# Reordering the layers stage of a two-layer block: four shifts in a row, gate sums ahead of the last head turnings, the next norm's statistics behind them

## The reference, cut to what matters

```python
# layer 0: attention in segments of 512 tokens, each against every 8th key (64 keys), 16 heads of 16
q4 = q.reshape(B, H, S, SEG, hd)
k4 = k.reshape(B, H, S, SEG, hd)[:, :, :, ::DIL]
scores = jnp.einsum('bhspd,bhskd->bhspk', q4, k4)
c = jnp.max(scores.reshape(B, H, S, nb, BLOCK_M, Kn), axis=4, keepdims=True)   # over 64 queries
w = jnp.exp(scores - c)
out = num / den[..., None]            # num = w v, den = sum of w
# layer 0: gate, an fp8 linear layer of the same normed tokens
out = jnp.einsum('bsi,oi->bso', x_dq, w_dq) + bias
...
x = x + s * g
xn = _layernorm(x, axis=-1)
# layer 1: q, k, v projections; q and k are rotated
q_rot = jnp.concatenate([q1 * cos - q2 * sin, q1 * sin + q2 * cos], axis=-1)
```

## Time and profile before

| what | value |
|---|---|
| median of 3 runs | 3221.84 us |
| the profiled execution's own time | 3216.31 us |
| its span | 3214.5 us |
| mean granted TensorE clock, of full speed | 0.971 |
| PE, DVE, ACT, POOL busy, share of the span | 90%, 79%, 64%, 21% |
| layers stage, segments 2 to 15 | from 128.5 us, one every 41.0 to 41.1 us |

### The profile page before, as it was taken

How to read it: one execution, slowest core, us unless ns; L and a number is a source line. 1 busy time by engine, 2 the same in 40 slices (tenths; PEclk the granted TensorE clock), 3 DMA queues, 4 the chain that set the end, 5 groups by cost and what they waited for, 6 DMA issues and landing times. The chain is left out here.

```text
span 3214.5 us, 66525 instructions
## 1 busy us (share of the span) xinstructions
PE 2893.3 (90%) x26519; PEld 1757.1 (55%) x26520; DVE 2555.0 (79%) x3560; ACT 2044.4 (64%) x3430; POOL 674.3 (21%) x1035
## 2 busy tenths in 40 slices
PE   5888888872899999999999999999899999999987
PEld 3555555550334443344344434434388888888975
DVE  4888888877899999999999999999265665666567
ACT  2555555540699999999999999999732232333234
POOL 1333333341222322000000000000132343332300
PEclk9999999985899999999999999999999999999999
DMA  2223333325223112222220122202121222212349
GB/s 76 69 86 89 88 91 93 93 86 102 51 55 54 36 24 54 54 54 53 54 53 17 43 54 54 53 22 87 52 68 34 71 80 73 68 42 70 103 150 309
DMA packets 252583, 230.21 MB, mean 72 GB/s; under 512 B 60908, under 2 KB 234988, under 8 KB 252012
## 3 DMA queue, kind: packets, MB, share of 16 engines
q1 hardware_dynamic: 235896, 192.32, 22.9%
q0 software_dynamic: 16384, 33.64, 3.3%
HBM read 124.21 MB, written 101.06 MB: 70 GB/s over the span
## 5 line engine op out<-in xcount | busy, mean ns | idle before, releaser
L1746 ACT ACTIVATE at_ex<-at_so,keep_exp_scale 128x512 f32<-128x512 f32 (+1 forms) x2304 | 1336.3, 679 | 203.6 <-PE at_so L1582 115.8
L1784 DVE TENSOR_REDUCE at_best<-at_p 128x2 f32<-128x1024 f32 (+3 forms) x1280 | 1284.5, 1060 | 111.1 <-PE at_p L1602 80.9
L1621 PE MATMUL at_so<-at_qs,at_ks 50*128 50x512 f16 (+3 forms) x2560 | 734.3, 352 | 33.0 <-ACT at_ex L1746 32.6
L1602 PE MATMUL at_p<-at_ks,at_qs 48*128 48x512 f16 (+3 forms) x2560 | 681.4, 358 | 50.6 <-DVE at_best L1784 49.4
L1692 PE MATMUL at_so<-at_ex,at_vs 128*32 128x256 f32 (+2 forms) x8704 | 697.2, 392 | 0.0
L2020 ACT ACTIVATE e_hh<-e_hb,e_b1now 128x512 fp32r<-128x512 f32 x256 | 176.4, 689 | 519.0 <-PE e_hb L1954 504.6
L1621 PEld LDWEIGHTS at_so<-at_qs,at_ks 50*128 50x128 f16 x2560 | 208.2, 93 | 517.6 <-ACT at_ex L1746 339.4
L1257 POOL DMA_INDIRECT e_xg<-s_xn,e_token x128 | 143.4, 1121 | 1359.5 <-DVE e_token L1252 1235.0
L1984 PE MATMUL e_ob<-e_w2h,e_hh 128*128 128x256 f32 x1024 | 295.3, 288 | 15.1 <-DVE e_og L2091 15.1
L1986 PE MATMUL e_ob<-e_w2h,e_hl 128*128 128x256 f32 x1024 | 291.8, 285 | 0.0
L1985 PE MATMUL e_ob<-e_w2l,e_hh 128*128 128x256 f32 x1024 | 291.7, 285 | 0.0
(11 more groups left out here) (267 smaller groups left out, 4498.6 us busy)
## 6 DMA issues: line engine op xcount, KB each, us to landing
s_v<-a_v SPq DMA_DIRECT2D x64, 256.0 KB, 3.0
s_qk<-a_part SPq DMA_DIRECT2D x128, 128.0 KB, 2.4
at_vs<-s_v SPq DMA_DIRECT2D x32, 512.0 KB, 10.3
s_eo<-at_empty SPq DMA_DIRECT2D x16, 1024.0 KB, 7.6
e_w<-w SPq DMA_DIRECT2D x16, 1024.0 KB, 7.7
f_rows<-s_eo SPq DMA_DIRECT2D x32, 512.0 KB, 8.0
at_qs<-s_qk SPq DMA_DIRECT2D x96, 128.0 KB, 4.4
at_ks<-s_qk SPq DMA_DIRECT2D x96, 128.0 KB, 7.2
```

The costliest lines, as they stand in the source:

```text
L1602: last = pe.matmul(out, qs[rows, buf, p, qt * P:(qt + 1) * P], ks[rows, buf, p, ch * SEG:ch * SEG + w], start=True, stop=ch != qc)
L1621: last = pe.matmul(so[:, v % NST, at:at + w], ks[rows, r, p, kt * P:(kt + 1) * P], qs[rows, r, p, q0:q0 + w], start=True, stop=not diag)
L1746: ev.done(act.activation(ex[:, v % NE, 0:width], so[:, v % NST, 0:width], ACT.Exp, scale=keep["exp_scale"][:, 0:1]), "ex")
L1784: last = dve.tensor_reduce(best[:, row:row + PAIRS * TT + 1:PAIRS * TT, ch], p1[:, at % NP1, :, to:to + w], AX, ALU.max)
```

## The change: what it does

The diff moves steps in the hand-written orders of POOL, PE, ACT and DVE. No instruction is added or taken away, and no buffer, shape or semaphore changes.

- DVE: all four `shift`s come first; `quantise_rest` moves behind `normalise(m, 0)`; `low_tokens(n)` behind `normalise(m, 1)`; `gated(m, 0)` and `gated(m, 1)` each one `normalise` earlier; `first_norm(m + 1)` behind `normalise(m, 3)`, right ahead of `residual(m, 0)`.
- PE: `scores(m, 3)` ahead of `turn_second(n)`; `gate(m, 0)` and `gate(m, 1)` each ahead of a `turn`; `project1(n, 2)` ahead of `turn_first(m + 1)`.
- ACT: `second_turned(n)` from behind `out_copy(m, 0)` to behind the third exponential, ahead of `out_copy(m, 1)`; `projected(n, 1)` ahead of `first_normed(m + 1)`; `projected(n, 2)` ahead of `first_turned(m + 1)`.
- POOL: `rotate` waits for the first `shift` of segment `n + 2` in place of `quant`; `rest(m - 2)` comes ahead of `inverse_root(m + 1, 0)`.

```diff
--- before.py
+++ after.py
@@ -350,7 +350,7 @@
                     ev.wait(pool, "pjc", n, 4)
                     ev.wait(pool, "p2", n, 0)
                     if n + 2 < NSEG:
-                        ev.wait(pool, "quant", n + 2, 1)
+                        ev.wait(pool, "shift", n + 2, 1)
                     st.then(pool.tensor_tensor(rot[:, :, 1, :], qk[:, :, 0, :], sin, ALU.mult))
                     st.then(pool.tensor_tensor(prod1[:], qk[:, :, 1, :], cos, ALU.mult))
                     st.settle()
@@ -385,10 +385,9 @@
                 for m in range(NSEG):
                     if m >= 2:
                         rotate(st, m - 2)
+                        rest(st, m - 2)
                     if m + 1 < NSEG:
                         inverse_root(st, m + 1, 0, "var", "rstd", "xn")
-                    if m >= 2:
-                        rest(st, m - 2)
                     inverse_root(st, m, 1, "var1", "rstd1", "xn1")
                 rotate(st, NSEG - 2)
                 rest(st, NSEG - 2)
@@ -589,25 +588,25 @@
                     for d in range(3):
                         scores(m, d)
                     values(m, 0)
+                    scores(m, 3)
                     if n >= 0:
                         turn_second(n)
-                    scores(m, 3)
                     values(m, 1)
                     turn(m, 0)
                     values(m, 2)
                     turn(m, 1)
                     values(m, 3)
+                    gate(m, 0)
                     turn(m, 2)
-                    gate(m, 0)
+                    gate(m, 1)
                     turn(m, 3)
-                    gate(m, 1)
                     project1(n, 0)
                     turn_heads(m)
                     project1(n, 1)
                     project(m)
+                    project1(n, 2)
                     if more:
                         turn_first(m + 1)
-                    project1(n, 2)
                     values1(n, 0)
                     project1(n, 3)
                     if more:
@@ -745,10 +744,10 @@
                         ev.wait(act, "shift", m, d + 1)
                         ev.wait(act, "pv", m, max(2 * (d - 1), 0))
                         ev.done(act.activation(wexp[:, d % 2], shifted[:, d % 2], ACT.Exp, scale=SCALE), "wexp")
+                        if d == 2 and n >= 0:
+                            second_turned(n)
                         if d >= 1:
                             out_copy(m, d - 1)
-                        if d == 1 and n >= 0:
-                            second_turned(n)
                     if n >= 1:
                         part0(n - 1)
                     out_copy(m, 3)
@@ -756,14 +755,14 @@
                     half_tanh(m, 1)
                     projected(n, 0)
                     heads_turned(m)
+                    projected(n, 1)
                     if more:
                         first_normed(m + 1)
                     if m == 0:
                         high_weights()
-                    projected(n, 1)
+                    projected(n, 2)
                     if more:
                         first_turned(m + 1)
-                    projected(n, 2)
                     logits(n, 0)
                     projected(n, 3)
                     if more:
@@ -1002,19 +1001,19 @@
                     n, more = m - 1, m + 1 < NSEG
                     shift(st, m, 0)
                     shift(st, m, 1)
+                    shift(st, m, 2)
+                    shift(st, m, 3)
+                    normalise(st, m, 0)
                     quantise_rest(st, m)
-                    shift(st, m, 2)
-                    normalise(st, m, 0)
-                    shift(st, m, 3)
+                    normalise(st, m, 1)
                     if n >= 0:
                         low_tokens(st, n)
-                    normalise(st, m, 1)
+                    gated(st, m, 0)
+                    normalise(st, m, 2)
+                    gated(st, m, 1)
+                    normalise(st, m, 3)
                     if more:
                         first_norm(st, m + 1)
-                    normalise(st, m, 2)
-                    gated(st, m, 0)
-                    normalise(st, m, 3)
-                    gated(st, m, 1)
                     residual(st, m, 0)
                     if n >= 1:
                         rest(st, n - 1)
```

## The result

The changed kernel takes 3259.52 us, the median of 4 runs (3257.85 to 3267.98), beside 3221.58 us for the kernel before in 4 runs (3220.45 to 3222.61): 1.0123 times, 95% interval 1.0105 to 1.0142. It is slower, 37.9 us by the medians. My forecast was 3236 us with a range up to 3254: the direction was right, the loss was more than twice as large, and the time lies outside the range. It fits the rival in which the clock falls in every segment (3242 to 3262), which I had given 0.14.

What follows compares the result with a forecast made beforehand. No single engine full in the layers stage; PE sets the pace in a segment's second half. Segments +7.8, clock +11.7, ends -5.2 gave +14.3 us, so 3236 us; own range 3229 to 3243, whole range 3209 to 3254.

Steps and rivals of the forecast that it cites:

- the rival in which the clock falls in every segment: TensorE's clock falls in all 13 steady segments, 1.3 to 2.9 us each: 3242 to 3262 us; chance 0.14.
- The first half of a segment: Shifts through projection on DVE and PE: `x1` added from 24.87 in place of 27.78, 2.9 us won on this path.
- POOL's chain: Next norm's inverse root on POOL: DVE instructions with two SBUF inputs hold three of its instructions up; ready at 26.71.
- The clock: PE's 3.4 us gap ahead of `turn_first` lowers the clock: 1.3 us in 9 of 13 segments, +11.7 us.
- 0.60: Loss per segment at full clock: `keys` start at 31.85 in place of 31.25; 13 segments make +7.8 us.
- The ends: Segments 0, 1 and 15 gain 1.4, 1.2 and 2.6 us, together -5.2.
- the clock stays up: Rival: the gap ahead of `turn_first` costs no clock, only +7.8 - 5.2 = +2.6: 3224 us; chance 0.18.
- POOL isn't caught: Rival: the inverse root gets through between DVE's instructions: 3189, or 3213 if only line 945 is missed; chance 0.18.
- the rotation meets `quantise_rest`: Rival: POOL's rotation runs 0.8 later, DVE stands up to 2.4 us: up to +30, 3250 us; chance 0.04.
- open in the prediction: Whether line 853 (statistics, one SBUF input) holds POOL up: nothing to two waits of about 0.3 each; taken as nothing.

Runs made afterwards that it cites:

- e1: The changed kernel with DVE's `rest` of segment n-1 moved behind `second_norm`: 0.9937 times the kernel before, a steady segment 39.99 us.
- e2: The changed kernel with 12 extra matmuls on PE behind `project1(n, 2)`, filling the gap: 1.0023 times the kernel before, a steady segment 42.00 us.
- e3: The changed kernel with `first_norm(m + 1)` put back behind `low_tokens`, ahead of the gate sums: 0.9921 times the kernel before, a segment 39.94 us.
- e6: The kernel of e3 with POOL's rotation waiting for `quant` again: 3281.8 us in one run, segments 46.6 and 45.5 us in turn.
- e7: The kernel before with only POOL's rotation waiting for the first shift instead of `quant`, one run: a segment 44.37 us.
- e4: The kernel before with only `first_norm(m + 1)` moved behind `gated(m, 1)`: 1.0363 times the kernel before, segments 49.01 and 49.96 us in turn.

## Why the prediction was right or wrong

*The first half of a segment* came as predicted: the fourth shift with a wait of 0.22, the first normalise at 9.94 (said: 9.90), the first gate sum at 14.71 (14.6), the statistics at 17.75 (17.77), line 944 at 24.78 (24.87). Line 932 fell to 1.22 and gave nothing. The rotation lay beside the shifts at 2.37 each.

*POOL's chain* was right in its mechanism and in its size: the three instructions are caught, and the chain ends at 26.90 where I had 26.71, since line 944 came a little earlier and catches the eleventh instruction instead of the twelfth. e1 shows this cause by experiment, and segment 1 by itself: without the collision of line 972 the chain ends 2.0 us earlier, and so clear of line 944.

*The clock* is the step that failed. I took 1.3 us in 9 of 13 segments, 11.7 us; it is 2.4 us (e2: 44.37 less 42.00) in 13 of 13, about 31 us. Both factors were too small. The 1.3 was read from segment 1 of the kernel before. There TensorE was at 1.2 GHz for 3.4 us (101.8 to 105.2), over turnings and gate sums of which one had some 0.4 us to wait anyway; here it is at 1.2 GHz for 5.1 of the 5.44 us (granted clock 0.53) from `turn_first` to `keys`, and each of them counts. A price read from a shorter slow stretch somewhere else was the wrong one to carry over. The count was wrong as well: behind a gap of 3.7 us the clock fell in every steady segment of both traces of the changed kernel. A small part of the miss isn't the clock's: at full clock the way to `keys` takes 3.05 (e2), not 2.91. The sum with the measured terms is 0.60 + 0.18 (`turn_first` at 29.12 instead of 28.94) + 0.14 + 2.39 (5.44 less 3.05) = 3.31 us a segment, or 43.0 for 13 of them, against 43.3 measured. Of the 30.6 us by which the forecast falls short between the profiled executions (+14.3 against +44.9), 23.8 lie in these 13 segments and 6.8 in the ends.

*The ends.* I said -5.2. Segment 1 gained 2.4 (said 1.2), since its clock fall is gone too. The rest behind the start of segment 15 gained 1.4: the layers' part of it as I said (the first scores of the next stage start 96.2 after segment 15 instead of 98.7), but 1.1 of it was lost again in later stages, which the change doesn't touch. Segment 0 lost 3.9 where I said -1.4, and this is the second step that failed: I had put the clock's fall there at nothing, without a reason. It isn't a fixed cost: with the same order it took 41.55 and 38.26 in the two traces of the changed kernel, and its granted clock was 0.88 and 0.91. In the first, line 944 also caught POOL's last instruction (1.23), and PE stood 4.27 ahead of `turn_first`; in the second the chain was through and PE stood 1.70, but `project` took 5.26 instead of 3.72. In e3 and e6, with the statistics back, segment 0 took 34.5 at granted clock 1.00.

*The rivals.* That the clock stays up, that POOL isn't caught, and that the rotation meets `quantise_rest` all didn't happen; e7 shows the last at its price in the other order. The clock that falls in every segment did happen, at 2.4 us, inside the 1.3 to 2.9 that this rival had. I had the right mechanism among the rivals and gave it the smaller chance, since the kernel before showed one fall in 14 waits of 2.22.

## What to carry to other kernels

A chain of tiny instructions on GpSimd is easily stretched (from 3.74 to 6.63 us here): look at which VectorE instructions on large tiles in SBUF, above all those with two SBUF inputs, will lie beside it at its new place, not only at when its input is ready. If a move makes TensorE wait in one piece in each round, price what follows the wait at half the clock, in every round, if it lies on the path: waits of 3.2 to 6.0 us did this in each steady segment of the runs that have them, 1.7 did it in none (e1), and 2.2 did it in one kernel (e4) and not in another. And what is won ahead of the engine that sets the pace is worth nothing until its own last input comes earlier: here VectorE was 3 us ahead and the segment 3.3 us longer.

## What the hardware showed that I had not expected

Adding 12 matmuls (2.9 us of TensorE work) to each of 13 segments made the segments 2.37 us shorter, because they kept TensorE at 2.4 GHz (granted clock 1.00 instead of 0.92).

Statistics instructions (line 852, one SBUF input) don't hold GpSimd up: lines 340, 342 and 344 took 0.19 to 0.20 beside them, at 468.45 to 469.20. That was open in the prediction. The rule cited there from the Trainium skill (SBUF — State Buffer, Who interferes with whom), that a VectorE instruction with one SBUF input outside the two-port modes doesn't contend, agrees with these rows.

One SBUF input alone is no safe sign, though. In e1 three instructions of the second inverse root take 0.73, 0.64 and 0.52 instead of 0.20, and each ends 0.04 to 0.06 after line 870, 872 or 874, a `tensor_scalar` on 128x1024 with one SBUF input; in e3 line 870 and the two behind it do the same (0.52, 0.64, 0.53). No run here moves these lines away, so this is read from the rows only.

Three traces (the changed kernel twice, and e7) have steady segments of the same length, all but one between 44.34 and 44.46, though e7 has another order and other waits; e4 and e6 fall into two lengths in turn. All five have a fall of the clock in each steady segment. I have no experiment on why the lengths agree, and leave it open. It is a reason to take the 2.4 us as what the fall costs in this order and not as a constant.
